# Biased attention on one core: seven of sixteen score blocks get their bias from GpSimd, in SBUF

## What is computed

```python
q = _split_heads(queries @ Wq.T, N_HEAD, D_KEY)
k = _split_heads(keys @ Wk.T, N_HEAD, D_KEY)
v = _split_heads(values @ Wv.T, N_HEAD, D_VALUE)
scores = jnp.einsum('bhqd,bhkd->bhqk', q, k) * D_MODEL ** (-0.5) + attn_bias
weights = jax.nn.softmax(scores, axis=-1)
out = jnp.einsum('bhqk,bhkd->bhqd', weights, v)
```

## Time and profile before

| | |
|---|---|
| median of 3 runs | 2016.48 us (2015.81 to 2023.32) |
| the profiled execution | 2020.89 us |
| its span, first to last instruction | 2019.1 us |
| mean granted clock of TensorE | 0.947 |
| busy: TensorE, VectorE | 1857.6 us (92%), 1561.4 us (77%) |
| busy: ScalarE, GpSimd | 850.0 us (42%), 922.7 us (46%) |
| the biased stage, in the span | about 847 to 1908 us |

### The profile page before, as it was taken

One profiled execution on the slowest core, in us unless ns is written; L12 is line 12 of the kernel. 1 busy time (PEld: TensorE's weight loads), 2 busy tenths in 40 slices (PEclk: granted clock), 3 DMA queues, 4 the chain that ended last, 5 costly groups with the idle time before them and its releaser, 6 DMA issues. The chain is left out here.

```text
span 2019.1 us, 44426 instructions
## 1 busy us (share of the span) xinstructions
PE 1857.6 (92%) x17464; PEld 1283.8 (64%) x17466; DVE 1561.4 (77%) x2164; ACT 850.0 (42%) x1145; POOL 922.7 (46%) x434
## 2 busy tenths in 40 slices
PE   7999999999877969989999999999999999998737
PEld 4666656667547858866666666656666666666526
DVE  4666756667676446689999999998999999999683
ACT  3666756667430124424433343334433343333401
POOL 0355745566450024207555565546555565556300
PEclk9999999999878769999999999999999999999857
DMA  3000210000030033100000000120000000000100
GB/s 133 9 14 8 69 34 13 8 5 9 22 121 1 1 129 84 46 9 7 14 13 13 0 13 13 33 72 5 13 13 13 0 13 13 13 8 1 48 0 11
DMA packets 27756, 52.82 MB, mean 26 GB/s; under 512 B 4243, under 2 KB 15268, under 8 KB 27172
## 3 DMA queue, kind: packets, MB, share of 16 engines
q1 hardware_dynamic: 27216, 51.60, 7.8%
q10 hardware_dynamic: 468, 0.16, 0.0%
HBM read 51.23 MB, written 0.52 MB: 26 GB/s over the span
## 5 line engine op out<-in xcount | busy, mean ns | idle before, releaser
L345 POOL TENSOR_TENSOR biased_sums<-biased_sums,biased_scores 128x1024 f32<-128x1024 f32 x216 | 512.8, 2374 | 172.6 <-ACT biased_scores L647 155.8
L712 DVE TENSOR_TENSOR biased_scores<-ps,bias 128x1024 f32<-128x1024 f32 x256 | 311.1, 1215 | 57.6 <-PE ps L432 57.6
L726 DVE TENSOR_TENSOR ps<-ps,biased_scores 128x512 f32<-128x512 f32 x480 | 332.3, 692 | 4.1
L733 DVE TENSOR_TENSOR biased_scores<-biased_scores,ps 128x1024 f32<-128x1024 f32 x256 | 303.9, 1211 | 1.3 <-PE ps L490 1.3
L345 POOL TENSOR_TENSOR plain_sums<-plain_sums,plain_scores 128x1024 f32<-128x1024 f32 x104 | 247.1, 2376 | 81.5 <-ACT plain_scores L647 72.4
L432 PE MATMUL ps<-biased_queries,keys_again 64*128 64x256 f32 x2048 | 261.1, 391 | 13.6 <-DVE biased_scores L712 12.7
L647 ACT ACTIVATE biased_scores<-biased_scores 128x1024 f32<-128x1024 f32 x256 | 261.3, 1050 | 15.7 <-DVE biased_scores L733 14.7
L379 PE MATMUL ps<-weights_again,context_again 128*64 128x128 f32 x4096 | 248.8, 274 | 6.8 <-ACT keys_again L608 5.4
L379 PEld LDWEIGHTS ps<-weights_again,context_again 128*64 128x64 f32 x4096 | 226.3, 137 | 41.4 <-issue 24.6
L446 PE MATMUL ps<-biased_scores,biased_values 128*64 128x256 f32 x2048 | 246.0, 382 | 2.3 <-ACT biased_scores L647 1.7
L726 DVE TENSOR_TENSOR ps<-ps,plain_scores 128x512 f32<-128x512 f32 x240 | 167.4, 698 | 95.7 <-ACT plain_scores L630 90.8
(11 more groups left out here) (385 smaller groups left out, 2263.2 us busy)
## 6 DMA issues: line engine op xcount, KB each, us to landing
context<-in_ctx_t SPq DMA_DIRECT2D x8, 1024.0 KB, 5.7
context_again<-in_ctx_t SPq DMA_DIRECT2D x8, 1024.0 KB, 8.2
moe_w<-in_moe_w SPq DMA_DIRECT2D x32, 256.0 KB, 2.6
weights_again<-in_wqkv SPq DMA_DIRECT2D x45, 128.0 KB, 2.1
bias<-in_fside SPq DMA_DIRECT2D x1, 4096.0 KB, 17.4
biased_w_out<-in_w_out SPq DMA_DIRECT2D x16, 256.0 KB, 2.6
weights<-in_wqkv SPq DMA_DIRECT2D x21, 128.0 KB, 2.1
plain_w_out<-in_w_out SPq DMA_DIRECT2D x8, 256.0 KB, 2.6
```

What stands on the lines that cost most here:

```text
L345: pool.tensor_tensor(both(SUM[:, :, :, :]), both((E[:, 0] if kp == 1 else SUM)[:, :, :, :]), both(E[:, kp, :, :, :]), ALU.add).then_inc(su ...
L712: dve.tensor_tensor(E[:, kp, :, :, :].rearrange("p (h t) n j -> p h t (n j)", h=2), scores_bank(kp).rearrange("p (h t n) -> p h t n", h=2, ...
L726: ins = dve.tensor_tensor(to, highest, E[:, kp, :, n, :], ALU.max)
L733: dve.tensor_tensor(at, at, c.ps[:, LOWER, :].rearrange("p (a j) -> p a j", a=HQ).unsqueeze(2) .to_broadcast([P, HQ, 2, P]), ALU.add).then ...
```

## The change

In the biased stage blocks 1, 3, 5, 7, 9, 11 and 13 (`RAW`) are no longer biased on the way out of PSUM. ScalarE copies them to `E` as they are; GpSimd then adds the bias in place (`add_bias`). Block 15 and the even blocks stay with VectorE. VectorE takes the maxima of two blocks at a time, at each odd kp: those of blocks kp - 2 and kp - 1. GpSimd adds the bias of block kp - 2 of the next pair ahead of sum kp of this pair. Semaphores: `raw_kept` counts ScalarE's copies, `bias_added` the adds, and the waits of TensorE and VectorE follow the engine that now does the block. In the plain stage `RAW` is empty.

```diff
+        raw_kept, bias_added = sem("raw_kept"), sem("bias_added")
+        RAW = tuple(range(1, NP - 1, 2)) if biased else ()
+        KEPT, NR = NP - len(RAW), len(RAW)
...
+        def scores_out_of(p, kp):
+            if kp in RAW:
+                return raw_kept, NR * p - NR * START + RAW.index(kp) + 1
+            return scores_kept, KEPT * p + (NP - KEPT) * START + kp + 1 - sum(n < kp for n in RAW)
+
+        def scores_ready(p, kp):
+            if kp in RAW:
+                return bias_added, NR * p - NR * START + RAW.index(kp) + 1
+            return scores_out_of(p, kp)
...
             @block.gpsimd
             def _(pool):
+                def add_bias(p, kp, attending):
+                    pool.wait_ge(raw_kept, scores_out_of(p, kp)[1])
+                    at = E[:, kp, :, :, :].rearrange("p (h t) n j -> p h t (n j)", h=2)
+                    bias = BIAS[:, :, kp * 2 * P:(kp + 1) * 2 * P].unsqueeze(1).to_broadcast([P, 2, 2, 2 * P])
+                    pool.tensor_tensor(at, at, bias, ALU.add).then_inc(bias_added, 1)
+
                 def sums(m, kps=NP):
                     for kp in range(1, kps):
+                        if kps == NP and kp - 2 in RAW:
+                            add_bias(m + 1, kp - 2, True)
                         pool.wait_ge(exp_done, NP * m + kp + 1)
...
+                for kp in RAW:
+                    add_bias(START, kp, False)
                 sums(START)
...
                     if kp >= 2:
-                        pe.wait_ge(scores_kept, NP * p + kp - 1)
+                        pe.wait_ge(*scores_out_of(p, kp - 2))
...
-                    act.activation(both(E[:, kp, :, :, :]), scores_bank(kp), ACT.Copy).then_inc(scores_kept, 1)
+                    act.activation(both(E[:, kp, :, :, :]), scores_bank(kp), ACT.Copy).then_inc(
+                        scores_out_of(p, kp)[0], 1)
...
-                            if not biased:
-                                scores_out(m + 1, 2 * g, attending)
-                                scores_out(m + 1, 2 * g + 1, attending)
+                            for kp in (2 * g, 2 * g + 1):
+                                if not biased or kp in RAW:
+                                    scores_out(m + 1, kp, attending)
                             piece_out(m, AFTER_SCORES[g])
...
                 def peak(p, kp, n):
                     if n == 0:
-                        dve.wait_ge(scores_kept, NP * p + kp + 1)
+                        dve.wait_ge(*scores_ready(p, kp))
...
-                        if scoring and kp > 0:
+                        if scoring and biased:
+                            if kp not in RAW:
+                                scores_out(m + 1, kp, attending)
+                            for late in (kp - 2, kp - 1) if kp % 2 else ():
+                                if late >= 0:
+                                    peak(m + 1, late, 0)
+                                    peak(m + 1, late, 1)
+                        elif scoring and kp > 0:
                             peak(m + 1, kp - 1, 0)
-                        if scoring and biased:
-                            scores_out(m + 1, kp, attending)
-                            if kp > 0:
-                                peak(m + 1, kp - 1, 1)
```

More of the change, by code:

```diff
@@ L404, in queries @@
                     if not (isinstance(p, int) and p == START):
-                        pe.wait_ge(scores_kept, NP * p)
+                        pe.wait_ge(*scores_out_of(p - 1, NP - 1))
                     for i in range(DC):
@@ L461, in sums_out @@
                     pe.wait_ge(summed, NP * m + NP)
-                    pe.wait_ge(scores_kept, NP * (m + 1) + NP - 1)
+                    pe.wait_ge(*scores_out_of(m + 1, NP - 2))
                     turn_sums(FOLD, True, True).then_inc(sums_turned, 1)
@@ L496, in project @@
                     if scoring:
-                        pe.wait_ge(scores_kept, NP * (m + 2))
+                        pe.wait_ge(*scores_out_of(m + 1, NP - 1))
                         pe.wait_ge(o_kept, m + 1)
@@ L714, in scores_out @@
                                       BIAS[:, :, kp * 2 * P:(kp + 1) * 2 * P].unsqueeze(1).to_broadcast([P, 2, 2, 2 * P]),
-                                      ALU.add).then_inc(scores_kept, 1)
+                                      ALU.add).then_inc(scores_out_of(p, kp)[0], 1)
                 def peak(p, kp, n):
                     if n == 0:
-                        dve.wait_ge(scores_kept, NP * p + kp + 1)
+                        dve.wait_ge(*scores_ready(p, kp))
                     highest = c.ps[:, PEAKS, :].rearrange("p (a j) -> p a j", a=HQ)
```

## The result

The changed kernel takes 2108.8 us (median of 4 runs, 2107.2 to 2111.6) against 2016.7: a ratio of 1.0451, 95% interval 1.0426 to 1.0476. It is 4.5% slower. The prediction was 2114.5 us, with a range of 2082 to 2155.

A forecast was written before the change was run, and what follows sets the result against it. TensorE bounds the kernel before the change, GpSimd's queue after it. 15 pairs at 6.0 us longer plus 0.6 for the half clock, less 1 in the first sweep, give +98 us: 2114.5 us, range 2082 to 2155.

The forecast's parts named there:

- GpSimd no longer fits: In a biased pair GpSimd gets 53.5 us of work against 51.8 us between its start and deadline.
- The price of an add: Each GpSimd bias add of 128x1024 was taken at 2.38 us, seven making 16.7 us a pair.
- that rival: Repeated bias dear on GpSimd: each add 0.77 us more, 5.4 us a pair, 2195 us; chance 0.10.
- S: The start of GpSimd's sum 1 in a biased pair, from which the prediction counts its times.
- the 13 other steps: GpSimd steps up to sum 15 where no sum follows the one it waits for: 2.44 us each, 31.7 together.
- From sum 15 to the turned peaks: VectorE's block 15 add and six maxima behind sum 15: 5.6 us with handing over, peaks turned at S + 61.4.
- the way over the fold: GpSimd's fold, 1.4 us after sum 15, then TensorE's 3.6 us to turning the peaks; 0.6 us slack.
- The half clock: TensorE's 1.2 GHz after idling some 4.5 us before the folded sums: 0.6 us a pair, bounds 0 and 3.1.
- these two covers: Part of the half clock's cost falls into TensorE's idle time itself, part into the 0.6 us of slack.
- the dear-clock rival: TensorE's clock falls at full price in each pair: 3.1 instead of 0.6 us, 2152 us; chance 0.12.
- ScalarE's waits: ScalarE's copies wait for GpSimd's sums, holding TensorE's next piece up some 0.6 us, swallowed by the stall.
- The faster rival: GpSimd keeps up, adds at 1.5 us each; a pair nears 63.2 us, -12 us, 2004 us; chance 0.05.

The follow-up runs named there:

- 1: Changed kernel without GpSimd's bias adds, the bias of seven blocks left out: 0.9994 of the time before the change, pairs of 63.87 us.
- 3: Changed kernel with three blocks (3, 7, 11) instead of seven given to ScalarE and GpSimd: 1.0016 of before, pairs of 63.87 us.
- 8: Changed kernel with one more GpSimd operation of 128x1024 ahead of sum 15 in each pair, result unread: 1.0593 of before, 2140.0 us.
- 9: Changed kernel with five blocks (1, 3, 5, 7, 9) moved, maxima interleaved as before the change: 1.0005 of before, pairs of 63.77 us.
- 10: Changed kernel with six blocks (1 to 11, odd) moved, maxima interleaved as before the change: 1.0171 of before, 2053.9 us.
- 7: Changed kernel with 10 unread matmul instructions before TensorE's fold wait, and maxima 13 and 14 ahead of block 15's score add: 1.0276 of before, 2073.1 us.
- experiment 6: Changed kernel with 10 unread matmul instructions, some 4.4 us, in front of TensorE's wait for the folded sums: 1.0339 of before, 2085.3 us.
- 11: Changed kernel with only two blocks (7, 11) moved, maxima interleaved as before the change: 0.9941 of before, 2004.6 us.
- 12: Changed kernel with only block 11 moved, maxima interleaved as before the change: 0.9969 of before, 2012.7 us.
- 2: Changed kernel with no block moved (RAW empty), only the new order of the maxima left: 1.0291 of before, 2078.5 us.

## Why the prediction was right

Its direction, its mechanism and its place held. Two terms of its sum were off, in opposite directions, so that the pair's 6.1 us came nearer to the predicted 6.6 than the terms did: that much is luck.

- **GpSimd as the bound.** "GpSimd no longer fits" is what 1, 3, 8, 9 and 10 show from five sides: with no adds, three or five the pair does not grow, with six it does, and one more than seven lengthens TensorE's wait by its own length.
- **The price of an add.** Taken at 2.38 us, measured at 2.37. The repeated bias costs GpSimd nothing; that rival falls.
- **From sum 1 to sum 15.** Start of the first add: S + 6.6 predicted, 1055.89 - 1049.24 = 6.65 measured. End of sum 15: S + 55.8 predicted, 1103.56 - 1049.24 = 54.3 measured. What was mis-sized is "the 13 other steps I take at 2.44, a gap of 0.06": the measured step is 2.33 (1055.89 to 1058.22), less than an operation's own 2.37. 13 x 0.11 = 1.4 us too much. A page of the Trainium skill, "GPSIMD Engine Reference", section 2.1, says that a core of GpSimd starts the next instruction as soon as its own share of the last is done; the steps of 2.33 us agree, and so do the 2.5 us where a sum waits for the one ahead.
- **From sum 15 to the turned peaks.** 5.6 us predicted, 1109.08 - 1103.56 = 5.5 measured; and that the way over the fold is nearly as long, 7 confirms (67.6 against 68.5, 0.9 us of slack where 0.6 was predicted).
- **From the turned peaks to the next sum 1.** 8.5 us predicted and kept at full clock (experiment 6: turned at 1102.60, next sum 1 at 1111.12). So the pair at full clock is 68.5 us (6), where 69.9 was predicted.
- **The half clock.** "I take 0.6, nearer to the lower end because of these two covers" was too little: 0.8 and 2.3 us in turns, 1.5 on the mean. The covers were there, but once the value piece and the queries were slow, TensorE was later than the peaks. The mechanism of the dear-clock rival was there in each pair, at half of its 3.1 us. The Trainium skill, "TensorE: Matmul & The Clock Gate" (Part 1, "What's actually happening"), has the engine fall to 1.2 GHz after idling; the trace agrees, with 0.53 to 0.74 of full speed ahead of each of the 15 reductions.
- **The sum.** Predicted 15 x 6.6 - 1 = 98; measured 90.9 - 2.6 = 88.3. The pair's 4.6 + 1.5 = 6.1 us in place of 6.0 + 0.6. The lower end that goes with 5.2 us a pair is 2016.5 + 15 x 5.2 - 1 = 2093, not 2090; nothing hangs on it.
- **The change of batch.** "The stall of 3.78 us at the change of batch stays as it is": the wait did, at 3.67, but the two key blocks behind it took 6.53 us instead of 5.35, and that pair grew by 7.9 us (77.5 against 69.6), where the ordinary ones grew by 6.1. Only this one pair shows it.
- **ScalarE's waits.** They came, up to 3.8 us in front of a copy, and they lengthen no pair, since the pair at full clock is explained without them (6). Without GpSimd's adds they do not come up at all (1).
- **The faster rival.** The adds took 2.37 us, not 1.5. But "about 0.7 us a pair" for VectorE's relief was right: 63.25 in 11 and 12.
- **What was not priced.** The new order of the maxima costs 0.55 us a pair even when GpSimd keeps up (1, 3). It eats up most of the gain that was in reach.

## What to carry to other kernels

An engine's slack is worth only what lies between its first input and the moment at which its last result is wanted: GpSimd was busy 37 of 64 us, but five more operations of 2.4 us fitted, not the eleven that 27 idle us suggest. Before giving work to an idle engine, lay its whole queue between those two points and count. And give only as much as removes the wait that is there: two blocks, with the maxima in their old order, gained 0.6% where seven lost 4.5%.

## What the runs showed of the hardware

- A wait of TensorE of about 2 us brings the half clock in one pair and not in another of the same kernel (six blocks: 2.17 and 2.18 us, clock 1.00 and 0.97 over the pair). Where it came it cost 1.5 to 1.6 us (2, 10). With a gap of 4.4 us filled by matmuls whose result nobody reads, the clock stayed at 1.00 (6).
- Operations of 128x1024 on GpSimd that do not wait for each other follow at 2.33 us from start to start, with 2.37 us shown for each, so their rows overlap a little; the starts are the surer measure, as the profile's ends on this engine are rough. A sum behind the one that it waits for starts 2.5 us after it.
- GpSimd and VectorE did not slow each other by more than 1%: GpSimd's sums take 2.37 us before the change and after it, its adds 2.37 too, although one input has a repeated dimension; VectorE's lowering takes 1.21 us in both, its score add 1.215 and 1.225.
- One float32 matmul instruction stands as two matmuls in the trace: 20 instructions as 40, in 8.75 us.
